# Graph attention, residual and layer norm on one core: a pair of 128-row tiles as the unit of the schedule, in place of one tile

## What is computed

```python
q, k, v = heads(x @ Wq + bq), heads(x @ Wk + bk), heads(x @ Wv + bv)   # 16 heads of 32
scores = einsum('bhqd,bhkd->bhqk', q, k) / sqrt(32)
scores = where(adj == 0, -inf, scores)
out = einsum('bhqk,bhkd->bhqd', softmax(scores), v)
y = x + out @ Wo + bo
return (y - mean(y)) / sqrt(var(y) + 1e-5)      # over the 512 features
```

## Time and profile before

| | |
|---|---|
| median of 3 runs | 885.58 us (884.72 to 888.23) |
| profiled execution, its own time | 887.87 us |
| span of the profile, first to last instruction | 886.0 us |
| mean granted TensorE clock | 0.994 |
| busy: PE, DVE, POOL, ACT | 98%, 60%, 54%, 34% |
| one slot in the middle of the kernel | 13.26 us |

### The profile page before, as it was taken

How to read it: one execution, slowest core, us unless ns; L and a number is a source line. 1 busy time by engine, 2 the same in 40 slices (tenths; PEclk the granted TensorE clock), 3 DMA queues, 4 the chain that set the end, 5 groups by cost and what they waited for, 6 DMA issues and landing times.

```text
span 886.0 us, 17845 instructions
## 1 busy us (share of the span) xinstructions
PE 866.7 (98%) x7308; PEld 696.1 (79%) x7308; DVE 531.7 (60%) x723; ACT 297.5 (34%) x420; POOL 477.8 (54%) x415
## 2 busy tenths in 40 slices
PE   8999999999999999999999999999999999999985
PEld 6778778778778778778778778778778778788864
DVE  4556656656656656656656656656556556566654
ACT  6532332332333333333333233233233233243310
POOL 2264565555564565565556565565555555556641
PEclk9999999999999999999999999999999999999998
DMA  8323334243243433424243243423324233233332
GB/s 307 121 72 83 125 87 137 68 134 93 71 140 85 125 85 87 124 84 138 72 138 84 73 137 86 126 82 96 117 81 139 74 87 93 67 90 94 96 84 72
DMA packets 50145, 91.89 MB, mean 104 GB/s; under 512 B 11280, under 2 KB 13328, under 8 KB 47888
## 3 DMA queue, kind: packets, MB, share of 16 engines
q1 hardware_dynamic: 50064, 90.75, 35.6%
HBM read 40.37 MB, written 16.78 MB: 65 GB/s over the span
## 4 chain that ended last, share of the span: by engine, by line
PE 91%; SPq 3%; DMA 2%; DVE 2%; ACT 1%; issue 1%; POOL 0%; POOLq 0%; DVEq 0%
PE psum_v L267 14%; PE psum_v L268 12%; PE psum_v L269 12%; PE psum_ot L367 7%; PE psum_s L352 7%; PE psum_k L269 6%; PE psum_k L268 6%; PE psum_k L267 6%; PE psum_y L386 6%; PE psum_y L390 6%; PE psum_y L387 6%; SPq L210 2%; DMA pt<-tr 1%; DVE tr L611 1%; PE psum_v L425 1%
## 5 line engine op out<-in xcount | busy, mean ns | idle before, releaser
L742 POOL TENSOR_TENSOR soft<-soft,top 128x1024 f32<-128x1024 f32 x64 | 122.0, 1906 | 256.5 <-DVE top L601 256.5
L618 DVE TENSOR_REDUCE total<-soft 128x16 f32<-128x1024 f32 x64 | 78.1, 1220 | 165.1 <-ACT soft L509 165.1
L183 POOL TENSOR_TENSOR soft<-soft,inverse 128x1024 f32<-128x1024 f32 x63 | 129.0, 2047 | 77.5 <-DVE inverse L621 77.5
L628 DVE TENSOR_TENSOR ot_lo<-psum_ot,ot_hi 128x512 fp32r<-128x512 f32 x64 | 44.3, 692 | 148.4 <-ACT ot_hi L517 148.4
L509 ACT ACTIVATE soft<-soft 128x1024 f32<-128x1024 f32 x64 | 67.9, 1061 | 150.8 <-POOL soft L742 150.8
L478 ACT ACTIVATE kt<-psum_k,bk_slot,in_slot 128x512 f32<-128x512 f32 x118 | 85.3, 773 | 89.2 <-PE psum_k L269 89.2
L267 PE MATMUL psum_v<-wv_hi,x_hi 128*128 128x512 f32 x256 | 107.3, 419 | 0.0
L269 PE MATMUL psum_k<-x_hi,wk_lo 128*128 128x512 f32 (+1 forms) x268 | 101.5, 379 | 0.0
L268 PE MATMUL psum_k<-x_lo,wk_hi 128*128 128x512 f32 (+1 forms) x268 | 101.4, 378 | 0.0
L267 PE MATMUL psum_k<-x_hi,wk_hi 128*128 128x512 f32 (+1 forms) x268 | 101.1, 377 | 0.0
L269 PE MATMUL psum_v<-wv_hi,x_lo 128*128 128x512 f32 x256 | 101.0, 395 | 0.0
(11 more groups left out here) (93 smaller groups left out, 1436.8 us busy)
## 6 DMA issues: line engine op xcount, KB each, us to landing
pt<-tr SPq DMA_DIRECT2D x512, 64.0 KB, 2.0
row<-in_x SPq DMA_DIRECT2D x64, 256.0 KB, 2.9
out_rows<-row SPq DMA_DIRECT2D x64, 256.0 KB, 2.0
x_raw<-in_xt SPq DMA_DIRECT2D x15, 1024.0 KB, 5.5
adj<-in_adj SPq DMA_DIRECT2D x16, 128.0 KB, 2.3
qt<-in_wq SPq DMA_DIRECT2D x4, 256.0 KB, 4.9
x_raw<-in_xt SPq DMA_DIRECT2D x4, 256.0 KB, 5.4
kt<-in_wk SPq DMA_DIRECT2D x4, 256.0 KB, 6.9
```

The source lines that it names most:

```text
L183: ops.tensor_tensor(by_head(soft[:, c % 2, :]), by_head(soft[:, c % 2, :]), inverse[:, c % 2, :].unsqueeze(2).to_broadcast([P, HEADS, NODES]),
L742: nc.gpsimd.tensor_tensor(by_head(soft[:, c % 2, :]), by_head(soft[:, c % 2, :]), top[:, c % 2, :].unsqueeze(2).to_broadcast([P, HEADS, NO ...
```

## The change

The slot becomes a pair of tiles, a = 2p and b = 2p + 1. On PE pair p is: mix(a-2), mix(b-2), score(a), score(b), then eight projections in the order v(a), k(a+4), q(a+4), y(a-2), v(b), k(b+4), q(b+4), y(b-2). There are 30 such pairs (`FULL`); pair 0 and the last four tiles have lists of their own. The last group's q and k are no longer cut into units, and the `keep_warm` at the end goes.

`pt`, `ot_hi` and `ot_lo` get two buffers, the small row statistics get four. `x_raw` goes from two buffers to one. The four PSUM banks beside `psum_s` become a ring: which bank a product uses rotates with the pair, and PE waits for the reader of the bank before it writes.

`tr` goes. `mask` now writes `soft` with the two halves of the 64 keys apart: (block, head, key in block). The row maximum and the sum run over two axes of that, the two POOL operations broadcast over runs of 32, and the transpose works in place on the whole buffer. The DMAs read `soft` itself, and `mask` of two tiles later waits for them.

The end on PE, with T = 64: score T-4, T-3; mix T-6, T-5; v T-4, T-3; score T-2, T-1; y T-6, T-5; v T-2, T-1; mix T-4, T-3; y T-4, T-3; mix T-2, T-1; y T-2, T-1. SP then places T-4, loads row T-3, and places T-3, T-2 and T-1.

The lists of DVE, POOL, ACT and SP follow the pair. On DVE the two splits of mixed rows (`split_ot`) stand in front of the two masks. SP loads the residual row of tile b between the placing of tile a and that of tile b.

```diff
 # PE
+            project_k(3)
+            pe.wait_ge(k_done, 3)
+            project_v(0)
+            score(0)
+            score(1)
+            pe.wait_ge(k_done, 4)
+            project_k(4)
+            pe.wait_ge(k_done, 2)
+            project_q(4)
+            pe.wait_ge(v_done, 1)
+            project_v(1)
+            pe.wait_ge(k_done, 5)
+            project_k(5)
+            pe.wait_ge(q_done, 5)
+            project_q(5)
+            for p in range(1, FULL):
+                a, b = 2 * p, 2 * p + 1
+                pe.wait_ge(v_done, a)
+                mix(a - 2)
+                pe.wait_ge(k_done, a + 4)
+                mix(b - 2)
+                score(a)
+                score(b)
+                pe.wait_ge(q_done, a + 4)
+                project_v(a)
+                wait_for(pe, row_added, a - 2)
+                project_k(a + 4)
+                pe.wait_ge(ot_lo_done, a - 1)
+                project_q(a + 4)
+                pe.wait_ge(ot_lo_done, a)
+                project_out(a - 2)
+                pe.wait_ge(v_done, a + 1)
+                project_v(b)
+                pe.wait_ge(k_done, b + 4)
+                project_k(b + 4)
+                pe.wait_ge(q_done, b + 4)
+                project_q(b + 4)
+                pe.wait_ge(row_added, a - 1)
+                project_out(b - 2)
...
 # DVE, pair p (p >= 2)
+                add_row(a - 3)
+                split_ot(a - 2)
+                split_ot(b - 2)
+                mask(a)
+                mask(b)
+                read_v(a)
+                norm_row(a - 3)
+                sum_up(a)
+                sum_up(b)
+                turn(a)
+                turn(b)
+                add_row(a - 2)
+                read_v(b)
+                norm_row(a - 2)
 # POOL
+                make_rstd(a - 3)
+                centre(a)
+                centre(b)
+                add_bo(a)
+                normalise(pool, nc.gpsimd, a)
+                normalise(pool, nc.gpsimd, b)
+                if a + 2 * GT < TILES:
+                    split_x(a + 2 * GT)
+                if p % 2 == 0:
+                    make_bias(p // 2 + 1)
+                make_rstd(a - 2)
+                add_bo(b)
+                if b + 2 * GT < TILES:
+                    split_x(b + 2 * GT)
 # ACT
+                read_ot(a - 2)
+                read_ot(b - 2)
+                exp(a)
+                exp(b)
+                for c in (a, b):
+                    if c + 2 * GT < TILES:
+                        split_x(c + 2 * GT)
+                    read_k(c + GT)
+                    read_q(c + GT)
 # SP
+                if p % 2 == 0:
+                    load_adj(p // 2 + 1)
+                    if p // 2 + 2 < GROUPS:
+                        load_x(p // 2 + 2)
+                store(a - 3)
+                place(a)
+                load_row(b)
+                place(b)
+                store(a - 2)
+                load_row(b + 1)
...
 # DVE, the mask and the transpose
-                wait_for(dve, turned, T - 1)
+                if 2 <= c < TILES - 2:
+                    dve.wait_ge(pt_in[c % 2], 8 * DMA * (c // 2))
                 nc.vector.tensor_tensor(
-                    by_head(soft[:, c % 2, :]),
-                    psum_s[:, c % 2].rearrange("p b (h k) -> p (b h) k", k=NODES),
-                    bias[:, c // GT % 2, c % GT, :].unsqueeze(1).to_broadcast([P, HEADS, NODES]),
+                    soft_of(c),
+                    psum_s[:, c % 2].rearrange("p r (h b k) -> p (r h) b k", b=2, k=SQ)
+                    .rearrange("p h b k -> p b h k"),
+                    bias[:, c // GT % 2, c % GT, :].rearrange("p (b k) -> p b k", k=SQ).unsqueeze(2)
+                    .to_broadcast([P, 2, HEADS, SQ]),
                     ALU.add).then_inc(masked, 1)
...
-                wait_for(dve, pt_done, 8 * DMA * T)
-                nc.vector.transpose(tr[:, :, :, :].rearrange("p b h q -> p h b q"),
-                                    by_head(soft[:, c % 2, :])).then_inc(turned, 1)
+                flat = soft_of(c).rearrange("p b h k -> p (b h k)")
+                nc.vector.transpose(flat, flat).then_inc(turned, 1)
```

More of the change, by code:

```diff
@@ L136, in attention_kernel @@
[L136 to L149, removed]
@@ L359, in mix, with score @@
-            def mix(i, c):
-                T = 8 * i + c
-                pe.wait_ge(pt_done, 8 * DMA * (T + 1))
-                pe.wait_ge(v_done, T + 1)
+            def score(c):
+                buf, t = c // GT % 2, c % GT
+                wait_for(pe, masked, c - 1)
+                for kc in range(KC):
+                    if t == 0:
+                        pe.wait_ge(q_done, c + kc + 1)
+                        pe.wait_ge(k_done, c + kc + 1)
+                    if kc == 0 or t == 0:
+                        pe.sem_inc(pe_went_on, 1)
+                    for graph in range(2):
+                        rows = slice(t * P + graph * NODES, t * P + (graph + 1) * NODES)
+                        for pair in range(2):
+                            f = slice(pair * 2 * DH, (pair + 1) * 2 * DH)
+                            last = nc.tensor.matmul(
+                                psum_s[graph * NODES:(graph + 1) * NODES, c % 2, pair,
+                                       kc * 2 * NODES:(kc + 1) * 2 * NODES],
+                                qt[f, buf, kc, rows],
+                                kt[f, buf, kc, 2 * t + graph, :, :].rearrange("p s k -> p (s k)"),
+                                start=True, stop=True)
+                last.then_inc(scored, 1)
@@ L364, in mix @@
+            def mix(c):
+                pe.wait_ge(pt_in[c % 2], 8 * DMA * (c // 2 + 1))
+                pe.wait_ge(v_done, c + 1)
                 pe.sem_inc(pe_went_on, 1)
@@ new lines, in _ @@
+            T = TILES
+            score(T - 4)
+            score(T - 3)
+            pe.wait_ge(v_done, T - 4)
+            mix(T - 6)
+            pe.wait_ge(k_done, T)
+            mix(T - 5)
+            pe.wait_ge(q_done, T)
+            project_v(T - 4)
+            pe.wait_ge(row_added, T - 6)
+            project_v(T - 3)
+            score(T - 2)
+            score(T - 1)
+            pe.wait_ge(ot_lo_done, T - 5)
+            project_out(T - 6)
+            pe.wait_ge(ot_lo_done, T - 4)
@@ L573, in _, with split_x @@
+            for c in range(T - 4, T):
+                exp(c)
+            for c in range(T - 4, T):
+                read_ot(c)
         @block.vector
         def _(dve):
-            def split_x(i, c):
+            def split_x(c):
                 buf, rows = c // GT % 2, slice(c % GT * P, (c % GT + 1) * P)
-                dve.wait_ge(x_hi_done, 8 * i + c + 1)
-                nc.vector.tensor_tensor(x_lo[:, buf, :, rows], x_raw[:, buf, :, rows],
+                dve.wait_ge(x_hi_done, c + 1)
+                nc.vector.tensor_tensor(x_lo[:, buf, :, rows], x_raw[:, :, rows],
```

750 lines of the change are left out of this document (339 added, 411 removed).

## The result

The changed kernel takes 895.58 us (893.55 to 896.49), the kernel before 886.5 (now over four runs): 1.0105 times as long, 95% interval 1.008 to 1.0129. So it is **slower by 1.05%**, above the range of the prediction, and by the mechanism of the rival "the placing of b becomes the bound". The profiled execution took 893.55 us, with a span of 891.8.

A forecast was written before the change was run, and what follows sets the result against it. PE was taken as the bound. Start 57.2, clock 1.7, 29 pairs 754.6, landings 1.5 and end 56.4 gave 871.4 us of span; with 1.87 around it and 2.3 off for the profiled execution, 871.0 us, range 862 to 891.

The forecast's parts named there:

- the placing of b becomes the bound: Rival, chance 0.25: chain from mix(b-2) to mix(b) leaves PE waiting; 29 us for each us beyond the slack.
- PE's work in a pair: Middle of the kernel: fewer changes of matmul kind save 0.50 of 26.52 us, so a pair takes 26.02.
- the rival of 0.19 per pair: Rival, chance 0.12: each small set on PE keeps its price, only 0.19 saved per pair; 880 us.
- The forms: DVE and POOL operations over runs of 32: DVE 0 to 0.05 each, POOL 0 to +1.3 for two; taken as 0.
- The start: First tiles: mix(0) at 52.4, mix(1) at 58.1, pair 1 as if begun at 57.2 us, plus a clock cost.
- the 1.7: Start: us lost to a lowered PE clock after the 4.7 us idle gap; bounds 0 and twice that.
- The chain behind normalise(a): In each pair, turn(a), SP's placings and load of row b: mix(b) can start at 26.85 us.
- exp(a) (1.06) and sum(a) are done by 10.5 and wait for nobody.: Softmax of tile a in each pair: these two operations add no delay before normalise(a).
- a slack of 0.1: Each pair: mix(b) can start at 26.85 and PE comes there at 26.94 us; the slack was 3 before.
- The allowance of 1.5 us for disturbed transfers: All pairs together: cost of late DMA landings, the worst of 3.6 us costing 1.6 for each pair hit.
- The end: From score(60) to the end: 54.4 us plus 2.0 for the clock, together 56.4.
- 2.0 us that I had allowed for the clock: End: cost of a lowered PE clock after idle gaps of 4.6 and 2.8 us; bounds 0 to 4.

The follow-up runs named there:

- alternate: The changed kernel with PE's short sets in the order score, mix, score, mix and DVE's masks before its splits: 885.7 us, 1.0012 of the kernel before.
- small_norm: The changed kernel with every second row normalised in only 8 of its 512 columns: 887.84 us, 1.0012 of the kernel before.
- norm_early: The changed kernel with `norm_row(a-3)` moved between the two `split_ot` on DVE: 889.81 us, 1.0051 of the kernel before.
- end_rstd: The changed kernel with POOL making rstd of T-4 and T-3 ahead of `add_bo` of the last two rows: 890.73 us, 1.0053 of the kernel before.
- scores_on_pe_only: The changed kernel with both scores before both mixes on PE, DVE's order unchanged: 910.95 us, 1.0276 of the kernel before.

## Why the prediction was wrong

Right, by its own steps:

- **PE's work in a pair.** 26.02 was predicted and is 25.96. Mix after mix and score after score cost nothing extra; alternate prices the changes that went at 0.16 each, which refutes the rival of 0.19 per pair. The Trainium skill's rule ("TensorEngine Tiling (Array Packing)", section Tiling Modes, Key Properties) that a change of mode drains TensorE agrees with these 0.16.
- **The forms.** No operation whose form changed grew by more than 0.03; normalising is 0.13 shorter.
- **The start.** mix(0) at 52.9 and mix(1) at 58.5 (52.4 and 58.1 predicted), the granted clock 0.62 there and 0.89 after, pair 2 at 85.05 (84.9). The 0.4 us by which mix(1) was late and a clock cost 0.3 below the 1.7 nearly cancel.
- **The chain behind normalise(a)**: 12.20 predicted from the placing of a to mix(b), 12.10 measured.

Wrong:

- **"exp(a) (1.06) and sum(a) are done by 10.5 and wait for nobody."** This step failed. I had left `norm_row(a-3)` out of the chain, as a short operation under POOL's work. It stands ahead of sum(a) on DVE's list, and beside centre(b) it waits for POOL. normalise(a) came 0.44 us later than I had it. small_norm shows that 1.51 of its 1.77 us are not its own work on the columns; norm_early, which moves it away, takes 0.56 off the chain. With a slack of 0.1 that alone made the chain the bound: 26.32 per pair instead of 26.02, 8.4 us in 28 pairs. A rule that would have warned me stands in the Trainium skill, "GPSIMD Engine Reference", section Specifications: GpSimd's SBUF interfaces are shared with VectorE, with contention for VectorE's 2-port modes and for instructions with two SBUF inputs. The trace agrees that the two contend (1.77 beside POOL's operation, 0.55 alone); that `norm_row` runs in such a mode no trace here shows. The form with two tensor inputs behaves in the same way (2.03 beside, 0.75 alone). For how long it waits the runs show: until POOL's operation ends.
- **The allowance of 1.5 us for disturbed transfers.** I looked at landings, whose worst was 3.6, and not at issues. The single long issues cost 0.28 a pair, 7.8 us. They were there before too (10 over 0.9 us, in sum 7.4 us beyond the usual 0.6 each; after the change 14 and 10.6), hidden under the 3 us by which pt was early. The term was mis-sized because the cover went together with the slack.
- **The end: 56.4 predicted, 62.0 measured.** I followed pt and not POOL's list. end_rstd gives back 3.5 of the 5.6. The rest has no run of its own; mix(62) starts 39.3 us after score(60) where I had 36.5, and y(60) ahead of it ran at a granted clock of 0.53 (859.5 to 864.0 us), against 2.0 us that I had allowed for the clock.

The rival had the right mechanism and place, and its price of 29 us per us is near the 28 pairs that paid. By my own sum (an estimate) the undisturbed chain alone, 0.30 us per pair, leaves the kernel at about 879: the long issues and the end made it slower than before. What I had against it, that every nearest row has the same price, was true and beside the point: the chain also holds operations that no edit touched.

**Left open.** Why a packet of instructions lengthens an issue on another queue or delays a landing, why the packets fall on the placing of b so often in scores_on_pe_only, and whether PE's stops are a lack of instructions, are not shown; the coincidence is. Nor does the trace tell for certain whose program q8 carries.

## What to carry to other kernels

When a change leaves a slack of 0.1 us in a chain, list every instruction of each engine's queue that stands in it, those untouched by the change too, and give each the price it has beside its new neighbours: a VectorE operation that meets a GpSimd one can last as long as that one, as `norm_row` did here and the maximum did not. Slack is also what hides single long DMA issues; a chain without it pays for each. The four short sets in a row were worth keeping, but with the scores first, so that the longest way round the engines does not begin at the last thing PE does.

## What was unexpected in the hardware

- A VectorE operation of 8 columns lasted 1.51 us beside GpSimd's 1.92 us operation, one of 512 columns 1.77, and 0.55 alone. Whatever was left of GpSimd's operation, the one of 512 columns ended 0.28 us after it. POOL's next operation suffered as well: `add_bo` took 1.48 right behind, and 1.30 in norm_early.
- SP's issues of 0.6 us take 0.9 to 2.2 us now and then, some 2% of them, almost only when a 16 KB packet of instructions starts just before them or during them. Transfers issued around such a packet landed after up to 3.9 us, and not 2.0.
- PE stood still for 2.75 us inside a set of 64 matmuls with nothing to wait for, at the same instruction in two kernels, and it was gone in a kernel with 40 instructions more.
